# A decoder on one core: the packing transfers of both cross attentions write every third partition

## The reference

```python
def _L1_xattn_ref(Q, K, V, Wq, bq, Wk, bk, Wv, bv, Wo, bo):
    q = _split_heads(Q @ Wq.T + bq, B, S)        # 16 heads of 16 dimensions
    k = _split_heads(K @ Wk.T + bk, B, S)
    v = _split_heads(V @ Wv.T + bv, B, S)
    scores = jnp.einsum('bhqd,bhkd->bhqk', q, k) * scale
    probs = jax.nn.softmax(scores, axis=-1)
    out = jnp.einsum('bhqk,bhkd->bhqd', probs, v)
    return out.transpose(0, 2, 1, 3).reshape(B, S, D) @ Wo.T + bo
```

## Time and profile before

| | us |
|---|---|
| median of 3 runs | 2904.79 (2891.71 to 2907.19) |
| the profiled execution, its own time | 2915.71 |
| its span, first to last instruction | 2913.0 |
| cross attention 0, in the span | about 466 to 960 |
| cross attention 1, in the span | about 2200 to 2690 |
| mean granted TensorE clock | 0.917 of full speed |

### The profile page before, as it was taken

The page is one execution under the profiler, slowest core; times in us unless marked ns, Lnnn a source line. Parts: engine busy times, 40 slices in busy tenths (PEclk is TensorE's granted clock), DMA queues, the critical chain, the costliest instruction groups (busy, mean ns, idle before and its releaser), DMA issues. The chain is left out here.

```text
span 2913.0 us, 50682 instructions
## 1 busy us (share of the span) xinstructions
PE 2441.5 (84%) x17441; PEld 2058.2 (71%) x17442; DVE 1916.7 (66%) x5065; ACT 1129.9 (39%) x2063; POOL 996.4 (34%) x1326
## 2 busy tenths in 40 slices
PE   4999996899998699999999999957674988985770
PEld 3888874566665699999999999946563666654770
DVE  6999972576775566666666665546553677776458
ACT  2566552455554222221222222212461655553550
POOL 3555541111111362233321330055111244445664
PEclk7999997899999799999999999978886999987895
DMA  2244103446441200013121120021004646540436
GB/s 69 96 143 143 34 1 71 69 70 121 68 66 20 95 35 29 29 65 106 38 72 66 35 72 29 29 71 57 7 0 75 88 97 131 70 63 2 141 117 243
DMA packets 170626, 206.26 MB, mean 71 GB/s; under 512 B 21061, under 2 KB 148847, under 8 KB 170480
## 3 DMA queue, kind: packets, MB, share of 16 engines
q1 hardware_dynamic: 139680, 154.58, 23.2%
q0 software_dynamic: 15360, 23.63, 2.8%
q10 hardware_dynamic: 15440, 26.22, 2.6%
HBM read 95.42 MB, written 77.20 MB: 59 GB/s over the span
## 5 line engine op out<-in xcount | busy, mean ns | idle before, releaser
L1576 PE MATMUL m_gu<-m_x_hi,m_w_hi 128*128 128x256 f32 x1632 | 462.6, 283 | 18.0 <-issue 10.5
L1576 PE MATMUL m_gu<-m_x_hi,m_w_lo 128*128 128x256 f32 x1632 | 458.5, 281 | 0.0
L1576 PE MATMUL m_gu<-m_x_lo,m_w_hi 128*128 128x256 f32 x1632 | 458.4, 281 | 0.0
L1613 ACT ACTIVATE m_sg<-m_gu 128x256 f32<-128x256 f32 x408 | 157.5, 386 | 671.4 <-PE m_gu L1576 654.0
L1647 DVE TENSOR_TENSOR m_h<-m_sg,m_gu 128x256 f32<-128x256 f32 x408 | 171.6, 421 | 290.2 <-ACT m_sg L1613 287.4
L1106 ACT ACTIVATE x_pt<-x_ps 128x1024 f32<-128x1024 f32 x256 | 262.6, 1026 | 226.5 <-PE x_ps L934 221.6
L1576 PEld LDWEIGHTS m_gu<-m_x_hi,m_w_hi 128*128 128x128 f32 x1632 | 309.9, 190 | 22.0 <-issue 11.9
L1576 PEld LDWEIGHTS m_gu<-m_x_hi,m_w_lo 128*128 128x128 f32 x1632 | 310.1, 190 | 0.0
L1576 PEld LDWEIGHTS m_gu<-m_x_lo,m_w_hi 128*128 128x128 f32 x1632 | 309.8, 190 | 0.0
L1208 DVE CUSTOM_DVE_ANT_0 x_ps<-x_ps,x_mb 128x256 f32<-128x256 f32 x512 | 201.7, 457 | 119.2 <-PE x_ps L934 119.1
L1565 PE MATMUL m_yp<-m_w_hi,m_h_hi 128*128 128x256 f32 x816 | 239.9, 294 | 4.5 <-DVE m_h_lo L1649 4.5
(11 more groups left out here) (320 smaller groups left out, 5634.7 us busy)
## 6 DMA issues: line engine op xcount, KB each, us to landing
yt<-zero SPq DMA_DIRECT2D x8, 2048.0 KB, 10.7
x_qpack<-x_qh SPq DMA_DIRECT2D x128, 128.0 KB
x_kpack<-x_kh SPq DMA_DIRECT2D x128, 128.0 KB
m_yr<-yt SPq DMA_DIRECT2D x16, 1024.0 KB, 13.2
m_x<-xs SPq DMA_DIRECT2D x36, 256.0 KB
ys<-m_y SPq DMA_DIRECT2D x35, 256.0 KB, 2.2
xs<-zero SPq DMA_DIRECT2D x8, 1072.0 KB, 6.0
m_x<-xs SPq DMA_DIRECT2D x32, 268.0 KB
```

Source lines behind the costliest of these rows:

```text
L1576: ins = pe.matmul(gu[:, m % 4, n, :], wp[n][:, c, m * P:m * P + P], xp_[:, c, :], start=(c == 0 and k == 0), stop=(c == KC - 1 and k == 2))
L1613: act.activation(sg[:, m % 4, :], gu[:, m % 4, 0, :], ACT.Silu).then_inc(silu_ready, 1)
```

## The change

The three parts of a dimension move next to each other. Part `part` of dimension `r` lay on row `16 * part + r` of a half; now it lies on row `3 * r + part`. Both tiles get the same order, so the same products are summed. The source, the bytes, the number of transfers, their order and all waits stay; row 48 stays.

```diff
             def pack(dst, n, part, src):
                 for m in range(KC):
-                    lo = 64 * m + DH * part
-                    sp.dma_start(dst[lo:lo + DH, n % PACKS].bitcast(F32),
+                    lo = 64 * m + part
+                    sp.dma_start(dst[lo:lo + 3 * DH:3, n % PACKS].bitcast(F32),
                                  src[:, m, :].bitcast(F32)).then_inc(pack_loaded[n % PACKS], 16)
```

## The result

| | before | after |
|---|---|---|
| median of 20 runs, us | 2905.13 (2891.71 to 2916.62) | 2891.68 (2884.72 to 2900.49) |
| ratio after / before | | 0.9957 (0.9947 to 0.9968) |
| span of the profiled execution, us | 2913.0 | 2887.5 |
| mean granted TensorE clock | 0.917 | 0.919 |

The kernel is faster by 0.43%, 12.5 us by the ratio. The profiled executions lie 25 us apart; the profile of before was one of its slower ones, and not all of that difference belongs to the change. From TensorE's first query projection to the first issue of maxima, the profile after is 6.0 us shorter in the masked stage (41.4 for 47.4) and 5.8 in the unmasked one (37.8 for 43.6); the rest of the 25 lies elsewhere.

The account below looks back on a forecast made before the run. TensorE sets the pace, with late packing transfers, limited by their 16 neighbouring destination partitions, reaching it in three waits. Gains of 3.9 + 2.2 + 2.0 = 8.1 us take the median from 2904.79 to 2897, range 2882 to 2910.

Parts of the forecast that it names:

- The transfer: One 128 KB packing transfer, 1.06 us in bursts before, takes 0.67 us at 195 GB/s with every third partition.
- second rival: Packing transfers: the fullest group has 3 rows for 4, so 0.79 us each; gain 5.7 us, time 2899; chance 0.20.
- The first rival: Packing transfers: sources or handling of 1 KB packets limit them, 1.06 us and the waits stay; time 2905; chance 0.15.
- Term 1: First sequence of stage 1, unmasked: packed data end at 2220.2, a gain of 3.9 us (bounds 0 and 4.5).
- Term 2: First sequence of stage 0, masked: data end at 489.35 instead of 491.5, a gain of 2.2 us (bounds 0 and 2.5).
- Term 3: Middle of stage 1: the 1.65 us wait behind expert loads goes, with some clock loss; 2.0 of 3.0 us taken.
- The other periods: The 29 or so remaining periods: data land with 4.8 and 3.5 us of slack, so shorter transfers gain nothing.
- third rival: After stage 0's first wait, TensorE's clock returns earlier: 10 us more, 2887, or some 2880 with stage 1; chance 0.14.
- The slower pattern: Steady loop: strided writes collide more, deciding from 1.63 us a transfer; at 2.1 us the time is 3065; chance 0.04.

Follow-up runs that it names:

- the first alone: Every third partition only for the first sequence of each stage, later ones on neighbouring partitions, against the kernel before: 0.9979 (0.9963 to 0.9994), 6.1 us.
- the later-only kernel: Every third partition for all sequences but each stage's first, which keeps neighbouring partitions, against the kernel before: 0.9993 (0.9982 to 1.0004), 2.0 us.

## Why the prediction was right

2897 was forecast, a gain of 8.1 us of 2904.8. The median after is 2891.7, within the range of 2882 to 2910, and the gain is 9 to 13 us, larger than forecast. The mechanism is the one named: the destination's partitions limit a transfer, and only the waits of the earlier trace rows pay. Point by point:

- **The transfer.** 0.67 us was taken, 0.71 measured, and for the wrong reason; that the two lie so close is luck. The 195 GB/s of the first microsecond was read as a rate that the writes reach before they queue; the runs with every fourth partition show that it is about the rate of the issue. The full rate with every third is 160 to 175, about the 165 that the prediction named as the sign of its second rival, relief only by the fullest group. 0.71 comes of a start at the issue's rate (184 to 211 GB/s) and an end at the full one. So the rate was the rival's, and the transfer lies between the two. The first rival, a limit outside the destination, falls: only the destination changed, and the rate rose.
- **Term 1, 3.9 us:** 7.52 less 3.83 is 3.7.
- **Term 2, 2.2 us, the mis-sized one.** By the same subtraction 1.65 us here, but the profile of before was not typical at this place. Its key projection ran at half clock, 3.75 us for 8 matmuls, and the keys' issue came 5.6 us behind the queries'; after, it took 1.97 us, and the issue came 4.0 us behind, as in 10 of the 13 profiles. The data did not wait for the later keys; the queue stayed full, as in this window of the kernel before:

```profile
484.00:485.00 1.00, 1.00 (x5) 0.90 (x6) 0.00 (x0) 0.00 (x0) 1.00 (x1) 1.00 1.13 120
```

  So the first score came 14.9 us behind the queries' first issue in that profile, and as much (14.87 and 14.92) in the two experiments whose masked stage starts with the old layout and the usual 4.0 us. Their waits read 7.57 and 7.62 us in place of 5.79 because TensorE got there 1.8 us sooner. With the new layout the late issue of the keys would have set the end, and the forecast put it there. At the usual 4.0 us it doesn't: the score comes 11.2 to 11.45 us behind the queries, with a wait of 3.96 to 4.14. The gain is 3.5 us.
- **Term 3, 2.0 us:** 1.65 became 0.64 in the profile after and was absent in others; the experiments with the old layout there had 4.30 and 2.38. 1 to 4 us.
- **The other periods, nothing:** 2.0 us (a loss of 1.2 to a gain of 5.2), in which term 3 lies.
- **The clock.** 3.7 + 3.5 + 2.0 is 9.2 us, and 9 to 13 measured; up to 4 us are left, within the intervals. A part can be the clock. From TensorE's first score to the first issue of maxima in the unmasked stage is 23.4 us in all three profiles with the long wait there (2225.66 to 2249.07 before) and 21.3 in four of six with the short wait and every third partition or the first alone; the other two have 23.4. These are rows of the profile after, TensorE and then SP:

```profile
2215.55 1.99 PE L895 MATMUL x_ps<-x_cx,x_wqk 128*128 128x256 f32 x8
```

```profile
2230.09 1.52 SPq L813 DMA_DIRECT2D x_qpack<-x_nmT  x2
```

From 2208.78 to 2230.09 is 21.3 us. The 8 matmuls of 2215.55, at full clock here, took 2.84 us before, between the 1.99 of full and the 3.78 of half clock. That is 2 us in some executions, not the 10 of the third rival. In the masked stage the same distance is 24.5 us with the long wait and with the short, so there the clock gives nothing; the 27.1 us of the profile before were its own.

  The prediction named the clock in the three windows behind this stage's first wait as the test of its third rival. It was 0.50 in all three before and is 0.77, 0.57 and 0.75 after, which looks like that rival. But the later-only kernel, with the old layout and the long wait there, has 0.76, 0.58 and 0.74. The first windows of both, of the profile after and then of the later-only kernel:

```profile
492.00:502.00 10.00, 6.53 (x26) 4.19 (x27) 4.91 (x24) 3.13 (x8) 1.26 (x1) 0.77 0.30 80
```

```profile
497.00:507.00 10.00, 6.54 (x27) 4.17 (x25) 4.91 (x24) 3.13 (x8) 1.27 (x1) 0.76 0.31 80
```

  So the clock is up again in this stage without the change, and the third rival falls here. How much of the last microseconds the clock gives in the unmasked stage stays open.
- **The slower pattern** didn't show: a transfer of 0.71 us is far from the 1.63 from which it would decide.

## What to carry to other kernels

A transfer that is slower than its issue while its engines are full is worth a look at which partitions it writes: the same bytes on every third or fourth partition cost 0.71 or 0.62 us in place of 1.0. It pays only where something waits for the transfer, here in the first of each stage's 16 sequences and in one more, so over a third less DMA time became 0.4% of the time. Before a wait is sized from one profile, see whether the work ahead of it ran at its usual clock.

## What the runs showed of the hardware that was not expected

Partitions 32 apart seem to stand in each other's way as neighbours do. The prediction quotes the Trainium skill for it; no row of the kernel before showed it. With 16 neighbouring partitions, four rows to each group of four, the rate is 124 GB/s. Every third partition puts at most 2 rows into any group of four neighbours. If only those counted, an estimate from the 124 gives twice that rate, 248, and the issue at 211 would be the limit, as with every fourth. It ran at 160 to 175 GB/s with a share over 1.1, near the 165 that the same estimate gives for 3 rows, and 3 is the most that a group holds when the rows 32 higher are counted in. No run varied that distance alone, so this is argued and not shown. Clearing 6 tiles of 128 x 2048 on VectorE, 1.76 us each, cost nothing that the time shows.
